# A fused gated delta rule and mixture of experts on one core: a new order of work, an input stage cut into items, and the last solve on another engine

## The reference

```
qkv  = silu(causal_conv4(norm(x) @ W_qkv.T))        # 8 heads of q and k, 16 of v, width 64
beta = sigmoid(norm(x) @ W_b.T);  g = -exp(A_log) * softplus(norm(x) @ W_a.T + dt_bias)
for each token t and head:                          # S is 64 x 64
    S = S * exp(g_t);  S = S + k_t (v_t - k_t.S) beta_t;  o_t = q_t . S
x = x + (norm_weight * rmsnorm(o) * silu(norm(x) @ W_z.T)) @ W_out.T
h = rmsnorm(norm(x)) * norm_w;  p = softmax(h @ router.T);  the 4 best of 32 experts per token
x = x + h' + shared(h) + sum_k p_k * expert_k(h)
```

## Time and profile before

| what | value |
|---|---|
| time, 3 runs | median 1165.8 us (1162.67 to 1166.7) |
| the profiled execution | 1162.42 us by the same measure as the runs |
| its span in the trace | 1160.6 us, so 1.8 us lie outside it |
| PE, DVE, ACT, POOL busy | 84%, 60%, 42%, 55% of the span |
| opening, up to `pm` of pair 0 | 0 to 140.1 us |
| pairs, `pm` of pair 0 to `pm` of pair 7 | 140.1 to 823.4 us |
| end of pair 7, experts, final sum | 823.4 to 1160.6 us |

### The profile page before, as it was taken

One profiled execution on the slowest core, in us unless ns is written; L12 is line 12 of the kernel. 1 busy time (PEld: TensorE's weight loads), 2 busy tenths in 40 slices (PEclk: granted clock), 3 DMA queues, 4 the chain that ended last, 5 costly groups with the idle time before them and its releaser, 6 DMA issues.

```text
span 1160.6 us, 32029 instructions
## 1 busy us (share of the span) xinstructions
PE 971.9 (84%) x12359; PEld 826.5 (71%) x12359; DVE 696.9 (60%) x1703; ACT 489.6 (42%) x932; POOL 641.9 (55%) x783
## 2 busy tenths in 40 slices
PE   4876899989898988999789889974886989999970
PEld 3765788778787878878778877873784657777760
DVE  6378957667765865776585476668443444333338
ACT  5524445345453543545364354531522234444430
POOL 3041348858875885787688578645031115555550
PEclk8686888879778887988997697797778989999995
DMA  6737036649348654933956540111147234444429
GB/s 234 228 77 189 1 69 177 169 115 279 97 127 216 175 170 131 276 103 107 261 129 174 153 98 29 34 39 37 69 202 285 92 96 132 129 131 129 128 47 359
DMA packets 181826, 165.33 MB, mean 142 GB/s; under 512 B 75427, under 2 KB 174124, under 8 KB 180784
## 3 DMA queue, kind: packets, MB, share of 16 engines
q10 hardware_dynamic: 72208, 73.96, 22.5%
q1 hardware_dynamic: 101840, 72.47, 21.3%
q0 software_dynamic: 7632, 16.87, 4.5%
HBM read 65.76 MB, written 101.55 MB: 144 GB/s over the span
## 4 chain that ended last, share of the span: by engine, by line
PE 43%; POOL 15%; DVE 14%; issue 10%; DMA 4%; another core or an unknown queue 2%; ACT 2%; SPq 1%; POOLq 0%; DVEq 0%; ACTq 0%
PE ps L1531 5%; POOL arena L785 5%; POOL arena L782 5%; PE ps L1615 4%; DVE arena L1119 4%; PE ps L1396 3%; POOL nrm L748 3%; PE ps L1548 3%; PE ps L1450 3%; PE ps L1460 3%; PE ps L1606 2%; PE ps L1429 2%; PE ps L1440 2%; PE ps L1406 2%
## 5 line engine op out<-in xcount | busy, mean ns | idle before, releaser
L1119 DVE SCALAR_TENSOR_TENSOR arena<-ps,cw,arena 128x256 f32<-128x256 f32 x384 | 155.4, 475 | 42.8 <-ACT arena L907 42.5
L1396 PE MATMUL ps<-work,arena 128*128 128x259 f32 x512 | 159.7, 469 | 15.4 <-DVE arena L1119 9.2
L1396 PEld LDWEIGHTS ps<-work,arena 128*128 128x128 f32 x512 | 116.5, 236 | 41.7 <-DVE arena L1119 10.4
L837 POOL DMA_INDIRECT picked<-work x95 | 93.4, 984 | 94.8 <-issue 48.7
L826 POOL DMA_INDIRECT slotted<-hr,slots x64 | 63.7, 996 | 102.6 <-DVE slots L1270 86.4
L785 POOL TENSOR_TENSOR arena<-arena 128x31 f32<-128x31 f32 (+15 forms) x186 | 111.1, 597 | 14.6
L1303 DVE TENSOR_TENSOR work<-work,ps 128x128 f32<-128x128 f32 (+1 forms) x111 | 34.0, 307 | 138.7 <-ACT work L1018 113.3
L1615 PE MATMUL ps<-arena,work 128*128 x380 | 101.3, 389 | 6.1 <-issue 5.0
L782 POOL TENSOR_TENSOR arena<-arena 128x31 f32<-128x31 f32 (+15 forms) x186 | 96.0, 516 | 12.4
L907 ACT ACTIVATE arena<-ps,cw 128x256 f32<-128x256 f32 x128 | 58.1, 470 | 76.6 <-PE ps L1396 60.7
L807 POOL TENSOR_TENSOR work<-work,ec 128x512 f32<-128x512 f32 x32 | 33.7, 1053 | 101.7 <-PE ps L1489 82.5
(11 more groups left out here) (224 smaller groups left out, 2262.6 us busy)
## 6 DMA issues: line engine op xcount, KB each, us to landing
slotted<-blank ACTq DMA_DIRECT2D x17, 4128.0 KB, 18.9
arena<-in_w SPq DMA_DIRECT2D x2, 6528.0 KB, 27.3
arena<-tab SPq DMA_DIRECT2D x96, 128.0 KB, 4.0
work<-slotted SPq DMA_DIRECT2D x95, 129.0 KB
arena<-picked SPq DMA_DIRECT2D x16, 512.0 KB, 9.5
work<-tab SPq DMA_DIRECT2D x32, 128.0 KB, 3.7
arena<-in_w_qkv SPq DMA_DIRECT2D x1, 2048.0 KB, 7.5
xin<-in_x SPq DMA_DIRECT2D x16, 128.0 KB, 4.8
```

Source lines behind the costliest of these rows:

```text
L837: g.indirect_dma_start(out=picked, out_offset=bass.IndirectOffsetOnAxis(ap=to, axis=0), in_=yrow[:, j % SLOTS, :], in_offset=None, bounds_ ...
L1119: v.scalar_tensor_tensor(out=acc_, in0=bank_of("proj", p, s_, i)[:, k:k + W2], scalar=cw[:, u, k:k + 1], in1=acc_, op0=ALU.mult, op1=ALU.a ...
L1396: ins = mm(to[:, 0:WX], wqkv[:, k, m:m + P], xt2[:, p % 3, k, :], start=k == 0, stop=k == KD - 1)
```

## The change

Three things are changed; what is computed and with which instructions stays the same, but for the banks of one intermediate.

1. The input stage is no list of its own. It is cut into items per engine (`stats` on DVE, `center`, `keepx` and `gate_a` on ACT, `turnx`, `ab` and `gate_p` on PE, `gate_d` on DVE), with numbers in a table OPENING, and sorted with everything else. `ab`, the decays and betas, is done in three parts, each as soon as its part of x is turned. GATES and HELD are gone. x is turned through three PSUM banks instead of four, since the fourth now holds the result of `ab`.
2. All tables are new, PAIR is 90.83 instead of 93.38, and pairs 0 and 1 have tables of their own (FIRST_0, FIRST_1), as the last two have.
3. `at_edge` names pair 0 alone: the solve of pair 7 is on POOL.

```diff
-PAIR = 93.38
+PAIR = 90.83
+OPENING = {
+    "stats": [(3.6, 0), (12, 1), (17.4, 2)],
+    "center": [(7.4, 0), (17.6, 1), (23.8, 2)],
...
+FIRST_0 = {
...
+    "blank": [(15.5,)],
...
+TABLES = (FIRST_0, FIRST_1) + (STEADY,) * (NP - 4) + (END_0, END_1)
...
-def opening():
-    out = [("norm", 0), ("turnx", 0)] + [("proj", 0, s, i) for s in range(2) for i in range(2)]
-    for g in range(1, len(GROUPS)):
-        out += [("norm", g), ("turnx", g)]
-        if g == 1:
-            out += [("mul", 0, s, i) for s in range(2) for i in range(2)]
-    return out + [(name, 0, s) for s in range(2) for name in ("tap", "sum", "silu")] + [("gate", 0)]
...
 def schedule():
-    timed = []
-    for p in range(NP):
-        table = STEADY if p < NP - len(ENDING) else ENDING[p - NP]
+    timed = [(t, (name, *ix)) for name, times in OPENING.items() for t, *ix in times]
+    timed += [(OPENING["tables"][0][0] + .1, ("ebload", n)) for n in (-2, -1)]
+    for p, table in enumerate(TABLES):
...
-    for item in first:
+    for _, item in sorted(timed, key=lambda e: e[0]):
         out.append(item)
-        while gates and gates[0][0] in out:
-            out += gates.pop(0)[1]
...
 def at_edge(p):
-    return p in (0, NP - 1)
+    return p in (0,)
...
+            def decays(g):
+                lo, hi = GROUPS[g]
+                pe.wait_ge(S["xt_out"], hi // 2)
+                pe.wait_ge(s_in, 48)
+                for n in range(2 * lo, 2 * hi):
...
-                    act.wait_ge(S["ab_mm"], 1)
+                    act.wait_ge(S["ab_mm"], len(GROUPS))
```

More of the change, by code:

```diff
@@ L199 @@
+    "base": [(196.5, 0), (233.2, 1)],
+    "hr": [(197.6, 0), (236.6, 1)],
+    "ht": [(198.6, 0), (237.9, 1)],
+    "htb": [(199.7, 0), (238.5, 1)],
+    "rt": [(200.3, 0), (239.1, 1)],
+    "mx": [(201.7, 0), (239.9, 1)],
+    "ex": [(202.5, 0), (240.6, 1)],
+    "tk": [(204.4, 0), (242.6, 1)],
+    "rank": [(207.1, 0), (245.3, 1)],
+    "slot": [(208.4, 0), (246.3, 1)],
+    "send": [(219.6, 0), (247.6, 1)],
+    "blanks": [(219.6, 0), (247.6, 1)],
 }
 END_1 = {
-    "dload": [(-48.4, 0), (-45.6, 1), (-41.7, 2), (-33.8, 3)],
@@ L314, in schedule @@
     out, step, before, ready = [], 0, {("oe", NC - 1), ("su", NC - 1), ("slot", NB - 3)}, {("base", NB - 3), ("au", NC - 1), ("su", NC - 1)}
-    planned = [item for _, item in sorted(timed, key=lambda e: e[0])]
-    head = opening()
-    moved, gates = set(head).union(*(then for _, then in GATES)), list(GATES)
-    first = head + [item for item in planned if item not in moved]
-    for item, cause in HELD.items():
-        if item in first and first.index(item) < first.index(cause):
-            first.remove(item)
-            first.insert(first.index(cause) + 1, item)
-    for item in first:
+    for _, item in sorted(timed, key=lambda e: e[0]):
         out.append(item)
-        while gates and gates[0][0] in out:
-            out += gates.pop(0)[1]
         before.discard(item)
```

430 lines of the change are left out of this document (259 added, 171 removed), and 201 rows, old and new, of tables (END_0, END_1, FIRST_0, FIRST_1).

## The result

The changed kernel takes 1187.5 us (median of four runs, 1180.99 to 1189.26) where the kernel before takes 1165.5: a ratio of 1.018, 95% interval 1.014 to 1.023, so it is **slower by 22 us**: clear of the noise, though the interval leaves open whether it is more than 2% or less. Its profiled execution has a span of 1179.3, 18.7 above the 1160.6 of before.

The account below looks back on a forecast made before the run. No engine alone was the bound (PE 43% of the chain); stages were summed, steady pairs counting five times. -8.2 + 7 - 23.5 + 8 - 2.6 = -19.3 from 1162.4 gives 1143.1, as a median 1146 us, range 1126 to 1167.

Parts of the forecast that it names:

- Covered: Waits on x's three banks and on clears: bank wait inside the opening's 6 late, clears cost 0, at most 3 per pair.
- my other end: Upper bound of the clears' cost: 3 us per pair, from waits that hold ACT; the forecast itself took 0.
- 45 to the solve and 51 back, 96: Steady pair: 45 us from `pm` to the solve, 51 from solve to `pm`, 96 for 100.7; five pairs give -23.5.
- rival A: `pm` to solve: PE keeps 2.4 GHz longer, pair 92.5, 1129 us; chance 0.16. Sign: denser order there, less PE idle, higher clock.
- Opening: Start to `pm` of pair 0: solve starts 4 late, five tap sets (12.2) leave it, `pm` 8.2 us earlier.
- Pair 0 to 1: Four projections and two `ss` come here from the opening: 100 us, +7, within 97 to 106.
- `send` out of the solve: Steady pairs, POOL: four indirect DMAs go behind the solve, taking 5.1 us off solve to `pm`.
- The 2.4 of turning and taps behind the solve: Between solve end and `pm` in steady pairs: the projection and taps there (2.44 of 6.47 us) can go.
- Added work between `pm` and the solve: Steady pairs: PE gets four projections and two `kt`, loses an `au` and a `ku`; 45 us, +2.9.
- Pair 6 to 7: Last solve on POOL +4.7, `pm` to solve +3.3; together +8, 94.5 us, bounds 86 and 99.
- Behind the last `pm`: After `pm` of pair 7, an `op` of 3.65 leaves PE's chain and a `v` of 1.02 enters: -2.6 us.
- D: Rival: between `pm` and solve, PE's added work runs at the low rate; steady pair 102.9, 1181 us, slower; chance 0.15.

Follow-up runs that it names:

- a_both: Changed kernel with the second scan behind L1294 on DVE and two of three 4 MB clears per pair issued later: 1159.9 us, ratio 1.005 to the kernel before.
- a_third: Changed kernel with second scan behind L1294, two clears later, third clear behind `tm`, and pair 1's second clear moved too: 1142.1 us, ratio 0.995 to the kernel before.
- a_scan: Changed kernel with only the second scan of the next pair put behind L1294 instead of ahead of it on DVE: 1178.2 us, ratio 1.011 to the kernel before.
- a_clear: Changed kernel with two of the three 4 MB clears of each pair issued later on ACT, scan left ahead of L1294: 1176.0 us, ratio 1.011 to the kernel before.
- a_open: Changed kernel with the first 4 MB clear behind ACT's first gate step instead of ahead of centring x's second part: 1180.0 us, ratio 1.023 to the kernel before.
- b_send: Kernel before with each pair's first `send` behind the solve, second `kb` and `ke` behind `tm`, second block's rows later, a clear moved too: 1213.3 us, ratio 1.041.
- a_last: Changed kernel with the solve of pair 7 on DVE again: 1186.8 us, ratio 1.031 to the kernel before.
- b_third: Kernel before with one clear of each steady pair moved from 79 behind `pm` to 3 ahead of the next `pm`: 1169.5 us, ratio 1.017.

## Why the prediction was wrong

**The step that failed is "Covered": "Clears: 17 before and after, each behind the last ... 0, with 3 per pair as its other end".** I had asked only whether ACT is held while it waits to issue a clear. In the steady pairs of the changed kernel it isn't (in the kernel before it was, for one clear in each steady pair, and not in pair 3 alone). What the clears do to others while in flight I had not asked, nor what stands behind a load that meets one; `dload` and `scan` have no term in the steady pairs at all. 4 MB take 17 to 24 us, and a clear is in flight for 0.53 of the time of the steady pairs (0.50 before). The new tables put the second load of a pair behind a clear and its scan ahead of L1294, and one of the three clears of a pair over `pm` and `tm`.

By the ratios, moving the scan and two clears brings 1.018 to 1.005 (a_both), and moving the third clear, with one more in pair 1, brings 1.005 to 0.995 (a_third). Together that is 24 parts in a thousand, 27 us, above the 15 of my other end for five pairs. The first step is the better shown. In a_third 4.0 stand between the last `nt` and L1294, for 8.9 in the changed kernel, and a_scan and a_clear each take away a part of it. The second step isn't of one cause. Its gaps of PE are a matter of place and not of amount: over the whole of the steady pairs the changed kernel has no more of them than the kernel before (last section).

Are the terms for the moved instructions right, then? In profiles it looks so. I had 45 to the solve and 51 back, 96; a_third has 45.7 and 47.2 + 3.5 = 50.7. But that is partly luck: it compares with a profile of the kernel before from 1162.4 us, and beside a_third that kernel took 1152.7. My forecast is a ratio of 0.983, and a_third, free of both losses, has 0.995 with 0.990 as the lower end. So some 14 us of the gain that I had forecast did not come even then, and no run shows which term they belong to. The granted clock is a part of the 96 as well. It is 0.87 from `pm` to the solve in a_third, 0.80 before, a sign that I had named for rival A.

Point by point:

- *Opening.* ACT held until 21.3: it was 21.5. The gate at 49: 49.6. `dload` at 71: 73.8. There were to be two sets of taps in the first solve, and 34.2 from its start to `pm`:

```profile
21.53 0.43 ACTq L1033 DMA_DIRECT2D slotted<-blank  x1
...
49.56 0.38 ACT L1004 ACTIVATE arena<-ps 128x256 f32<-128x256 f32 x1 [9.49 <-PE ps L1486]
```

```profile
73.83 6.24 SPq L771 DMA_DIRECT2D arena<-tab  x8
```

```profile
L1254 DVE SCALAR_TENSOR_TENSOR arena<-ps,cw,arena 128x256 f32<-128x256 f32 x12 | 4.9, 475 | 0.0
```

  The 12 instructions are there, and it took 33.7. What was too small is the delay of the solve: it began at 102.5, 9 late for my 4, so the gain is 3.9 for 8.2. My cause for the late gate was only a part of it: a_open shows that ACT would have stood there anyway, for projections.
- *Pair 0 to 1*, +3.9 for +7. PE was busy for 89.4 where I had 94 to 99.9: the granted clock was 0.93 in it, from 0.85. I had priced the added items by rows of either level and not the old ones at the new clock.
- *`send` out of the solve*, -5.1: the solve went from 51.5 to 45.8. With the `send` one `sd` (L807) of 1.0 left it as well, so the size fits, but the only run on the `send` alone (b_send) failed as a test. The 2.4 of turning and taps behind the solve came (7.0 to 4.7).
- *Added work between `pm` and the solve*, +2.9: in a_third +3.4, at a higher granted clock.
- *Pair 6 to 7*, +8.9 for +8, right by luck. I had the solve slower on POOL by 4.7; it took 43.6 (42.6 before on DVE), and `pm` to the solve grew by 8.7 instead of 3.3.
- *Behind the last `pm`*, -4.9 for -2.6. The sign held; I did not follow the rest.
- *Rivals.* D came closest in time: I had the steady pair at 102.9 by PE's added work at the low rate. The two projections between `pm` and `tm` do take 3.8, the low rate, but they take 3.8 in a_third too, where a pair is 96.4. So D's mechanism was not what cost most. A did not come about in the changed kernel: the clock from `pm` to the solve was 0.83 on the mean of the steady pairs, from 0.80. In a_third it was 0.87, and its first 11.4 us from `pm` had 0.70, from 0.57 in the 13.0 of before, so something of A may be in its time.

## What to carry to other kernels

When the order of work changes, large transfers that nobody waits for move too, and they are part of the change: for each, write down what is in flight with it before and after, small loads on the path above all, and stretches where an engine runs through many short instructions. A table of issue places beside the profile's DMA row is a start. Then ask of each prefetch whether the instruction that consumes it stands ahead of something that doesn't need it; in an in-order engine its lateness is passed on, and a_scan shows that moving it one place back mostly passes it on elsewhere.

And an edit is to be judged by the ratio to the old kernel run beside it. Here the old kernel itself differed by 1% from one group of runs to the next, and stages compared across profiles of different groups made the mended kernel look as good as the forecast, which it is not.

## What the runs showed of the hardware

PE can stand still in the middle of a run of equal matmuls while a 4 MB clear is in flight. The page of the profile lists the queue that brings instructions:

```profile
q8 instruction: 102, 1.67, 0.6%
```

102 packets and 1.67 MB are 16 KB each. In the trace each gap of PE can be set beside the packet of that queue that landed last. Five of them, with the gap, its end, and from the landing to the end, in us:

```
kernel    gap    ends     packet            end - landing
after     2.63   457.86   455.33 to 456.46   1.40
a_both    3.96   239.15   236.63 to 237.75   1.40
a_both    3.04   544.25   541.77 to 542.82   1.43
a_last    4.00   241.62   238.96 to 240.07   1.55
b_third   3.08   446.12   443.48 to 444.60   1.52
```

(The 0.84 in the expectation of a_third is the first of these, and should be 1.40.) Of 27 gaps of at least 0.78 at `pm` and `tm` in the steady pairs of these four kernels, 25 end 1.16 to 1.60 behind such a landing. A packet itself takes 1.1 on the median with a clear in flight and 1.0 without, so if a packet is late, it is by its start. At `pm` of pair 5 in b_third, where the gap is missing, packets of the queue began 0.2 ahead of `pm` and 7.1 behind it; at that of pair 3, where PE stood for 3.9 in all, they began at 4.7 and 12.7. So it also matters how much of a stock is left when the clear begins.

Such gaps are in the kernel before, too, at other places. One of them is in pair 3, under the first clear:

```profile
473.63 0.54 PE L1509 MATMUL ps<-work 64*64 64x128 f32 x5
475.95 0.77 PE L1509 MATMUL ps<-work 64*64 64x128 f32 x10 [1.78 <-issue]
```

Counted over the whole of the five steady pairs are gaps of at least 0.3 that end 1.1 to 1.8 behind a landing; there are 56 packets of the queue in them (55 to 56 in every kernel):

| kernel | gaps | us in all | of these in `pm` to `tm` |
|---|---|---|---|
| before | 7 | 10.5 | 0 |
| after | 6 | 8.1 | 7.6 |
| a_both | 13 | 23.7 | 18.4 |
| a_third | 10 | 18.0 | 0 |
| b_third | 14 | 28.6 | 15.6 |
| b_send | 0 | 0 | 0 |

The changed kernel has less of them than the kernel before, a_third, with its ratio of 0.995, has more, and b_send, with 1.041, has none. So the sum of the gaps says little about the time; what one costs depends on its place. In 49 of these 50 gaps a clear is in flight. That the next instructions come late behind the clear's packets fits all of this; that the queue shares the DMA engines in this way is an inference, which no run took apart further.

The Trainium skill, "Runtime: NRT & Kernel Launch", Instruction fetch mechanics, says that an engine's instructions are refilled in blocks of 16 KiB over a DMA queue of its own, and calls the cost mostly hidden. The packets agree with the first. "Mostly" agrees by count, as 49 of 56 packets before the change left no gap; but where one did, with a clear in flight, PE stood for up to 4.0 us.

The same clear makes a load of 128 KB take 14.71 in the chain above, where the page of the profile has a median of 4.1 for that load, and the third load takes 11.2 behind the clear and 3.2 in a_clear without it.
